# Two transformer layers on one core: the attention's key-value products and numerators as 32-wide array tiles, down scales split once, ranks and weights moved

## The reference, cut to what matters

```
# layer 0 attention: 16 heads of 32, linear
q, k = elu(x Wq^T) + 1, elu(x Wk^T) + 1;  v = x Wv^T
kv = sum_t k_t v_t^T (per head);  z = 1 / (q . sum_t k_t + 1e-6)
out = (q kv z) Wo^T
# layer 0 feed-forward: 4-bit weights, a float16 scale for each 128 inputs
h = silu(x Wg^T) * (x Wu^T);  y = h Wd^T;  y / rms(y)
# layer 1 attention: gated linear attention with one head of 32 keys, 64-step chunks
# layer 1 feed-forward: per batch the 512 best of 1024 tokens by a router's score go
# through a 2048-wide gelu feed-forward, weighted by sigmoid(score)
```

## Time and profile before

| | us |
|---|---|
| median of 3 runs | 1006.41 (1006.1 to 1541.61) |
| the profiled execution | 1005.34 |
| its span, first to last instruction | 1003.6 |
| TensorE busy | 928.8 |
| VectorE busy | 668.7 |
| ScalarE busy | 402.1 |
| GpSimd busy | 303.9 |
| mean granted clock of TensorE | 0.986 |

### The profile page before, as it was taken

How to read it: one execution, slowest core, us unless ns; L and a number is a source line. 1 busy time by engine, 2 the same in 40 slices (tenths; PEclk the granted TensorE clock), 3 DMA queues, 4 the chain that set the end, 5 groups by cost and what they waited for, 6 DMA issues and landing times.

```text
span 1003.6 us, 12375 instructions
## 1 busy us (share of the span) xinstructions
PE 928.8 (93%) x4182; PEld 728.5 (73%) x4182; DVE 668.7 (67%) x1325; ACT 402.1 (40%) x673; POOL 303.9 (30%) x270
## 2 busy tenths in 40 slices
PE   7998999898899999999998998999989989999993
PEld 5786788776576786776776666686857768878883
DVE  4666752666998778778856876866676777455413
ACT  4543022222334444454546367554454244323220
POOL 1000100001676543443333412232215322633333
PEclk9999999998999999999999999999999999999997
DMA  8433101201000000000010020010200444231411
GB/s 281 143 99 108 43 22 42 74 11 54 17 16 17 1 1 1 1 1 0 1 42 1 0 95 1 1 43 1 85 1 23 126 136 123 68 126 42 148 63 42
DMA packets 41792, 52.64 MB, mean 52 GB/s; under 512 B 5889, under 2 KB 23681, under 8 KB 41729
## 3 DMA queue, kind: packets, MB, share of 16 engines
q1 hardware_dynamic: 39904, 47.63, 14.7%
q0 software_dynamic: 1824, 4.22, 1.3%
HBM read 41.33 MB, written 10.50 MB: 52 GB/s over the span
## 4 chain that ended last, share of the span: by engine, by line
PE 42%; DVE 19%; issue 8%; ACT 4%; POOL 2%; DVEq 0%; ACTq 0%; POOLq 0%
PE ps_gla L41 10%; PE ps_gla L43 10%; PE ps_gla L42 10%; DVE acc L1543 9%; PE ps_gla L2127 4%; PE ps_gla L2128 4%; ACT acc L1257 1%; DVE junk L1729 1%; PE ps_gla L2227 1%; DVE router_junk L1697 1%; PE ps_gla L2157 1%; ACT fjunk L791 1%; PE ps_gla L2213 1%; DVE gsg L1655 1%; DVE scale_lo L1532 1%
## 5 line engine op out<-in xcount | busy, mean ns | idle before, releaser
L1543 DVE SCALAR_TENSOR_TENSOR acc<-ps_gla,gu_scale,acc 128x512 f32<-128x512 f32 x264 | 196.3, 749 | 64.9 <-ACT acc L1257 42.6
L2127 PE MATMUL ps_gla<-xt_hi,gu_val 128*128 128x512 f32 x352 | 147.3, 418 | 18.0 <-DVE acc L1543 7.0
L2128 PE MATMUL ps_gla<-xt_lo,gu_val 128*128 128x512 f32 x352 | 139.8, 397 | 0.0
L2127 PEld LDWEIGHTS ps_gla<-xt_hi,gu_val 128*128 128x128 f32 x352 | 67.2, 191 | 59.1 <-DVE acc L1543 40.7
L1257 ACT ACTIVATE acc<-ps_gla,gu_scale 128x512 f32<-128x512 f32 x88 | 60.5, 688 | 114.4 <-PE ps_gla L2128 114.4
L2034 POOL TENSOR_TENSOR fsg<-fsg,acc 128x512 f32<-128x512 f32 x44 | 62.1, 1412 | 129.3 <-DVE acc L1543 129.3
L616 POOL TENSOR_TENSOR a_rstd<-a_var,minus_half 128x1 f32<-128x1 f32 x16 | 10.8, 676 | 226.2 <-DVE a_var L508 226.2
L2128 PEld LDWEIGHTS ps_gla<-xt_lo,gu_val 128*128 128x128 f32 x352 | 67.5, 192 | 11.0
L2039 POOL TENSOR_TENSOR fh_lo<-fsg,fh_hi 128x512 fp32r<-128x512 f32 x44 | 56.8, 1291 | 51.8 <-ACT fh_hi L1269 51.8
L41 PE MATMUL ps_gla<-dn_hi,fh_hi 128*128 128x512 f32 x176 | 69.5, 395 | 0.0
L42 PE MATMUL ps_gla<-dn_hi,fh_lo 128*128 128x512 f32 x176 | 69.0, 392 | 0.0
(11 more groups left out here) (274 smaller groups left out, 2202.1 us busy)
## 6 DMA issues: line engine op xcount, KB each, us to landing
mw_raw<-in_w SPq DMA_DIRECT2D x16, 512.0 KB, 3.6
a_nib<-in_gate_up_packed SPq DMA_DIRECT2D x88, 64.0 KB, 2.2
x<-x SPq DMA_DIRECT2D x16, 256.0 KB, 3.6
mw_raw<-x SPq DMA_DIRECT2D x8, 512.0 KB, 4.4
out<-mw_raw SPq DMA_DIRECT2D x8, 512.0 KB, 3.0
xt_raw<-in_xT SPq DMA_DIRECT2D x3, 1024.0 KB, 5.1
x<-in_x SPq DMA_DIRECT2D x3, 1024.0 KB, 5.8
a_nib<-in_down_packed SPq DMA_DIRECT2D x8, 256.0 KB, 3.1
```

The source lines that it names most:

```text
L1543: dve.scalar_tensor_tensor(out=a[:, :], in0=ps[:, FG + c, :], scalar=gu_scale[:, part * IT + j, c:c + 1], in1=a[:, :], op0=ALU.mult, op1=A ...
L2127: pe.matmul(ps[:, FG + c, :], gu_val[:, o, c, :], xt_hi[b % 2][:, c, :], start=True, stop=False)
L2128: pe.matmul(ps[:, FG + c, :], gu_val[:, o, c, :], xt_lo[b % 2][:, c, :], start=False, stop=True).then_inc(s_gu, 1)
```

## The change

- Start: the k weights alone are loaded by SyncE, the v weights by four DMAs on ScalarE's queue; tokens 128 to 255 have a load and a split of their own; tiles 0 and 1 do their k halves, then their v halves; seven products of ones (`warm_up`) go ahead.
- `add_kv` multiplies each head alone: 16 products of 32 weight columns with 33 moving ones, one PSUM bank. The head mask goes; `sums` is one copy. `numerators(b, t)` does tiles t and t + 1, for each 16 products of 32 rows. `attend` has three instructions.
- Queries of half 1 are put between numerators, transposes and projections, on other banks (`Q_BANK`, `Y_BANK`, `q_next`).
- The down scales are split once, in the attention, on 11 partitions, stored to memory, and loaded as high and low rows, four slots of each; the nibble steps of block 0 are spread over six half iterations.
- In the last block of the second attention, ranks, scatters, `variance(2)`, `normalise(2)`, `router(2)`, `pair_weights(0)` and `lower_half(3)` have other places. The second attention's projections go to two banks in turn (`y_bank`), its transposes to one (`x_bank`).
- The last down products of tile 13 join those of 14 and 15. `feed_forward_to_end` clears its semaphores once, without a barrier.

```
-        kvz = put("a_kvz", [P, KC, P + HG], 200)
+        kvz = put("a_kvz", [P, KC, DH + 1], 200)
+        dn_scale16, dn_scale_hi, dn_scale_lo = (put(f"a_dn_scale_{name}", [IT, C], 148 + i, F16)
+                                                for i, name in enumerate(("all", "hi", "lo")))
...
+        q_next = [put(f"a_q_next{b}", [P, 2, BLK], (20, 108)[b]) for b in range(NB)]
+        v1 = [put(f"a_v1_{i}", [P, HEADS, DH + 1], 24 + i * 66 / 32) for i in range(2)]
...
-        KV0, YP, QP, TP, PROJ, FG = 0, 0, 2, 2, 4, 4
+        KV, TP, PROJ, FG = 0, 2, 4, 4
+        Q_BANK = ((2, 3, 2, 3), (2, 1, 0, 1))
+        Y_BANK = (1, 0, 0, 1, 0, 1, 0, 1)
...
-            for i in (WK, WV):
-                for c in range(KC):
-                    sp.dma_start(w_raw[i][:, c, :], wT[i][:, c, :]).then_inc(s_kvw[i][c], 16)
-            sp.dma_start(xt_raw[0][:, :, P:BLK], xT[:, :, P:BLK]).then_inc(s_xt[0], 16)
+            for c in range(KC):
+                sp.dma_start(w_raw[WK][:, c, :], wT[WK][:, c, :]).then_inc(s_kvw[WK][c], 16)
+            sp.dma_start(xt_raw[0][:, :, P:2 * P], xT[:, :, P:2 * P]).then_inc(s_x1, 16)
+            sp.dma_start(xt_raw[0][:, :, 2 * P:BLK], xT[:, :, 2 * P:BLK]).then_inc(s_xt[0], 16)
...
+            sp.dma_start(dn_scale16[:, :], dn_scales).then_inc(s_ds, 16)
...
+            sp.wait_ge(s_dsp, 2)
+            sp.dma_start(dn_parts[0], dn_scale_hi[:, :]).then_inc(s_dss, 16)
+            sp.dma_start(dn_parts[1], dn_scale_lo[:, :]).then_inc(s_dss, 16)
...
+            for c in range(KC):
+                act.dma_start(w_raw[WV][:, c, :], wT[WV][:, c, :]).then_inc(s_kvw[WV][c], 16)
...
+                if i == WK:
+                    act.wait_ge(s_x1, 16)
+                    act.activation(xt_hi[0][:, :, P:2 * P], xt_raw[0][:, :, P:2 * P], ACT.Copy).then_inc(s_x0h, 1)
...
-                kvp = ps[:, KV0:KV0 + 2, 0:2 * (P + 1)].rearrange("p a (g e) -> p a g e", g=2)
-                for a in range(2):
-                    dve.tensor_tensor(kvz[:, 2 * a:2 * a + 2, 0:P], kvp[:, a, :, 0:P],
-                                      const.head_mask[:, :].unsqueeze(1).to_broadcast([P, 2, P]), ALU.mult)
-                    ins = dve.tensor_tensor(kvz[:, 2 * a:2 * a + 2, P:P + HG],
-                                            kvp[:, a, :, P:P + 1].to_broadcast([P, 2, HG]),
-                                            const.head_mask[:, 0:P:DH].unsqueeze(1).to_broadcast([P, 2, HG]), ALU.mult)
-                ins.then_inc(s_kv, 1)
+                dve.tensor_copy(kvz[:, :, :], ps[:, KV, 0:KC * (DH + 1)].rearrange("p (g e) -> p g e", g=KC)).then_inc(s_kv, 1)
...
+                if i == 0:
+                    dve.wait_ge(s_dss, 32)
+                done(dve.tensor_scalar(z[:, :].rearrange("p (j g) -> p j g", j=HG), num[:, :, :, DH], 1e-6, None, ALU.add))
                 done(dve.reciprocal(zi[t % 2][:, :], z[:, :]))
-                for a in range(2):
-                    ins = dve.tensor_tensor(
-                        att[t % 2][:, 256 * a:256 * a + 256].rearrange("p (g h e) -> p g h e", g=2, h=HG),
-                        num[:, a, :, 0:P].rearrange("p g (h e) -> p g h e", h=HG),
-                        zi[t % 2][:, 8 * a:8 * a + 8].rearrange("p (g h) -> p g h", g=2).unsqueeze(3).to_broadcast([P, 2, HG, DH]),
-                        ALU.mult)
-                ins.then_inc(s_att, 1)
+                dve.tensor_tensor(att[t % 2][:, :].rearrange("p (g j e) -> p j g e", j=HG, e=DH), num[:, :, :, 0:DH],
+                                  zi[t % 2][:, :].rearrange("p (j g) -> p j g", j=HG).unsqueeze(3).to_broadcast([P, HG, KC, DH]),
+                                  ALU.mult).then_inc(s_att, 1)
...
+                queries(b, 1, 0)
                 attend(b, 0)
                 attend(b, 1)
                 att_low(b, 0)
+                att_low(b, 1)
+                queries(b, 1, 1)
+                queries(b, 1, 2)
                 attend(b, 2)
-                att_low(b, 1)
+                attend(b, 3)
...
+            def warm_up(count):
+
+                pe.wait_ge(const.steps, 1)
+                for _ in range(count):
+                    pe.matmul(ps[:, 3, 0:P], const.ones[:, :], const.ones[:, :], start=True, stop=True)
...
-                    ins = pe.matmul(ps[:, KV0 + g // 2, (g % 2) * (P + 1):(g % 2 + 1) * (P + 1)], k[n % 2][:, g * P:(g + 1) * P],
-                                    v1[n % 2][:, g, :], start=(n == 0 and g % 2 == 0), stop=(n == NT - 1), skip_group_check=True)
+                    for j in range(HG):
+                        h = HG * g + j
+                        ins = pe.matmul(ps[j * DH:(j + 1) * DH, KV, g * (DH + 1):(g + 1) * (DH + 1)], k[n % 2][:, h * DH:(h + 1) * DH],
+                                        v1[n % 2][:, h, :], start=(n == 0 and g == 0), stop=(n == NT - 1), skip_group_check=True)
...
-                for g in range(KC):
-                    ins = pe.matmul(ps[:, PROJ + 2 * (t % 2) + g // 2, (g % 2) * (P + HG):(g % 2 + 1) * (P + HG)],
-                                    q[:, g, col:col + P], kvz[:, g, :], start=True, stop=True)
-                ins.then_inc(s_num, 1)
+                for u in (t, t + 1):
+                    for g in range(KC):
+                        for j in range(HG):
+                            d = slice(j * DH, (j + 1) * DH)
+                            ins = pe.matmul(ps[:, PROJ + j, num_col(u, g)], query_out(b, h, g)[d, (u % TB) * P:(u % TB + 1) * P], kvz[d, g, :],
+                                            start=True, stop=True)
+                    ins.then_inc(s_num, 1)
...
+            warm_up(WARM)
             for b in range(NB):
-                tile_kv(b, 0)
-                if b:
-                    transpose_att(0, NT - 1)
+                if b == 0:
+                    for w in (WK, WV):
+                        tile_kv(b, 0, (w,))
+                        tile_kv(b, 1, (w,))
+                    add_kv(b, 0)
+                else:
+                    tile_kv(b, 0)
                     project_out(0, NT - 2)
                     project_out(0, NT - 1)
-                for n in range(1, NT):
+                for n in range(1 + (b == 0), NT):
                     tile_kv(b, n)
                     add_kv(b, n - 1)
                 query(b, 0, 0)
                 add_kv(b, NT - 1)
                 for m in range(1, KC):
                     query(b, 0, m)
+                query(b, 1, 0)
                 numerators(b, 0)
-                numerators(b, 1)
+                query(b, 1, 1)
                 transpose_att(b, 0)
+                transpose_att(b, 1)
+                query(b, 1, 2)
                 numerators(b, 2)
-                transpose_att(b, 1)
                 project_out(b, 0)
-                numerators(b, 3)
+                project_out(b, 1)
                 transpose_att(b, 2)
-                project_out(b, 1)
-                query(b, 1, 0)
                 transpose_att(b, 3)
                 if b:
                     for c in range(KC):
                         transpose_rows(c)
-                for m in range(1, KC):
-                    query(b, 1, m)
+                query(b, 1, 3)
...
-    ctx.callback(clear_semaphores, nc, sems)
+    ctx.callback(nc.clear_and_free_semaphores, sems)
...
-                if j >= 2:
-                    sp.wait_ge(s_s2, j - 1)
-                    sp.wait_ge(s_dh, j - 1)
-                sp.dma_start(scale[j % 2][:, :], dn_scales[j:j + 1, :].to_broadcast([P, C])).then_inc(s_scl[j % 2], 16)
+                i = j % SCALES
+                if j >= SCALES:
+                    sp.wait_ge(s_dl, j - SCALES + 1)
+                sp.dma_start(scale_hi[i][:, :], dn_parts[0, j:j + 1, :].to_broadcast([P, C])).then_inc(s_scl[i], 16)
+                sp.dma_start(scale_lo[i][:, :], dn_parts[1, j:j + 1, :].to_broadcast([P, C])).then_inc(s_scl[i], 16)
...
+                    if n == LAST and t == 1:
+                        pair_weights(0)
...
+            def nibble_step(u):
+                if u in (3, 5, 7):
+                    shift_nibbles((u - 3) // 2)
+                elif u in (4, 6, 8):
+                    mask_nibbles((u - 4) // 2)
...
                     if b == 0:
-                        down_scales(j)
-                        if 1 <= j < 1 + IT - DN_SLOTS:
-                            nibbles(j - 1)
+                        nibble_step(2 * j + 1)
...
-                    if n == LAST:
-                        rank(0, 3 + t)
                     if n:
                         residual(n - 1, t)
                     if t:
                         o_low(n, t - 1)
-                if 0 < n < LAST:
+                    if n == LAST:
+                        rank(0, 2 + t)
+                if n:
                     variance(n - 1)
                 o_low(n, TB - 1)
                 mean_square(n)
+                if n == LAST:
+                    rank(0, 6)
+                    rank(0, 7)
...
+                elif n == LAST:
```

(31 more changed lines are left out.)

280 lines of the change are left out of this document (149 added, 131 removed).

## The result

The changed kernel takes 962.37 us (median of four runs, 962.01 to 963.50); the kernel before, run beside it, 1006.88. The ratio is 0.956, with a 95% interval of 0.954 to 0.958: faster by 4.4%. One execution of the kernel before took 1541.61 us and is left out of the ratio; its median without it is 1006.41. I had forecast 990.5 and a range from 971 to 1027, so the result lies 28 us under the forecast and 9 under the range. The profiled execution took 962.24 us with a span of 960.3, 43.3 less than the span before.

A forecast was written before the change was run, and what follows sets the result against it. TensorE, busy 93% of the span, was taken as the bound, so time is won at its waits, low clock or work. Gains 29.7 less costs 13.8 give net 15.9: 1005.34 to 989.4 profiled, 990.5 median; range 971 to 1027.

The forecast's parts named there:

- Array tiles: add_kv and numerators: 32 short pairs in place of 8 cost 2.6 and 6.1 us, shape changes 3.6; 12.3 together.
- Rivals 1 and 2: Numerator loads go one after another, 1025, chance 0.17; pairs in add_kv and numerators have a 0.06 floor, 1015, chance 0.15.
- Moved ranks: Routing: earlier gather, waits for p_lo, rows and mw_lo ended, low clock gone; 8.5 us gained (4 to 10).
- Split scales: First feed-forward, block 0: two VectorE instructions fewer per iteration; 77.3 in place of 85.30 us, 8 gained (3 to 11).
- Middle: Middle of each attention batch: query products give cover; 8.5 of 10.2 us of TensorE waits ended (4 to 11.8).
- added wait: First attend: it waits until the split scales are stored to memory; 1.5 us cost, once (0 to 3).
- Start: Kernel start: k weights first, v on ScalarE's queue, products of ones ahead; 2.5 us gained of 6.7 waited.
- rival 4: Kernel start gains nothing, k and v sharing DMA engines whatever queue issues; 993; chance 0.5 together with the forecast.
- End: Kernel end: fewer last products ahead of the first finish, at most 0.7 us, and two barriers gone, 1.5.
- Rival 3: Tiles cheap, but half the waits return behind others (attention, block 0, loading): 15 gained, 13.8 spent, 1005; chance 0.18.

## Why the prediction was wrong

The sum was gains 29.7, costs 13.8, net 15.9. It came out as 43 gained. Step by step:

- **Array tiles, 12.3 of cost: the step that failed most.** For add_kv "nearest to the row of 64: I take 0.03", measured 0.012; for the numerators "0.04, near the end where the four go side by side", measured 0.030. I took the price of a load from loads that follow each other in the full array; the rows had nothing that lay side by side. The lower end of 0 for add_kv was wrong too: it gains 4.6. By starts the tiles gain some 2 in all, so this step is some 14 of the 27 us of error. Rivals 1 and 2 fall with it, though the first has a part of its mechanism on this chip: with the loop in the other order, 0.068 a pair (not its 0.111) and 35 us.
- **Moved ranks, 8.5: 13.3, and 2.0 more in the second feed-forward that I had at nothing.** Place right (gather, mw_lo, p_lo), size too small. The gather came 8.1 us sooner and not 4, and mw_lo's wait alone is worth 4.7 with what follows it. The granted clock falls twice in this stretch before, for 3.4 us each (from 795.5 and from 819.4), and not once in the changed kernel. One moved line, decays, I had not priced at all; putting it back costs 2.9.
- **Split scales, 8: 12.2 in block 0**, above my bound of 11. I left 3.4 us of nibble steps uncovered; iterations 1 to 4, which hold them, last 4.78, 7.33, 6.47 and 6.45 us where 16 and 28 products at 0.227 take 3.6 and 6.4, so 2.3 at most are uncovered. Most of the rest is that I built on block 1: its last six iterations take 43.9 in the kernel before, and the changed block 0's take 41.8. 9.9 of the first feed-forward's 12.6 come from the scales, 1.1 from the steps' new places.
- **Middle, 8.5 less the added wait 1.5, so 7.0.** The third and fourth row of the table gained 7.0 together, with 2.5 for numerators in tiles and 0.6 saved by two of the add_kv groups in it: 8.9 without the tiles, where I had 7.0, and 10.3 without the added wait too, where I had 8.5. The wait that I named as next, for the residual of row tile 1, did not show. The added wait cost 1.4 of the forecast 1.5, and where I put it. What made 10.3 of 8.5 is open: no run takes this order back as a whole. It was not the clock, since its granted share is 1.00 from 14 to 242 us in the kernel before.
- **Start, 2.5: 0.7**, in size as rival 4 has it. Its reason, the same DMA engines "whatever queue issues", is half of it: with v behind k on SyncE another 2.0 came, and with that the start would have gained 2.7, so the queue that I chose for v took back what I had forecast. 1.9 more came by the last key sums of batch 0, where the wait for a_k (1.64 at 30.22) ended, which my sum had left out. 0.9 was given back to the packed chunks, by the wait for a_q.
- **End, 2.2: 1.8.** Both terms as forecast, less 0.44 for the later last products.

Beneath the second and third lies one flaw: I priced a wait at its length, with the clock at most as a mean beside it. The kernels with one line put back measure 4.67 for a wait of 2.92, and 10 for two waits of 4.5 together; and block 0 lost time at starts that no list of waits has. Rival 3 held that half of the waits would come back; here ended waits in the routing and in block 0 took low-clock stretches with them. The bound of the range, 971, was named "tiles for nothing with all waits ended", but the better ends of my own terms add up to 42.2 (6.7, 11.8, 11, 10, 0.7 and 2) and, with no cost against them, to 964; the bound was added up wrongly as well.

## What to carry to other kernels

Price a TensorE wait of 2 to 3 us in a dense stream at its length and look for the products that start 0.43 apart behind it; add those, and count start-to-start intervals, not only rows marked with a wait. Give tiles of the array to small, masked or head-wise products when the loop goes round the row or column groups (and their banks) innermost, and look at the order before the size; that order was tried for the row groups alone. When a stage gets faster, see which queue of loads kept time with it before: here SyncE's series of issues, behind which an earlier start was worth nothing until the instructions that wait for it stood behind the queries.
